# Weighing the scans of two neighbouring Mamba units in one VectorE instruction over two PSUM banks

## The reference, cut to what matters

```python
def step(h, inp):
    dt_t, B_t, C_t, x_t = inp
    dA = jnp.exp(dt_t[..., None] * A)
    h = dA * h + (dt_t * x_t)[..., None] * B_t[:, None, :]
    y = jnp.einsum('ben,bn->be', h, C_t)
    return (h, y)
...
y = ssm_scan(dt, Bm, Cm, xc, A) + xc * Dp
y = y * jax.nn.silu(z)
return jnp.einsum('ble,de->bld', y, outproj)
```

## Time and profile before

| what | value |
|---|---|
| median of 3 runs | 2925.25 us |
| the 3 runs | 2925.6, 2925.25, 2921.18 us |
| span of the profiled execution, first to last instruction | 2927.1 us |
| mean granted TensorE clock over the span | 0.944 |
| busy: PE, DVE, ACT, POOL | 84%, 64%, 46%, 52% |
| weighings on VectorE (L581) | 624, 419.8 us |

### The profile page before, as it was taken

The page is one execution under the profiler, slowest core; times in us unless marked ns, Lnnn a source line. Parts: engine busy times, 40 slices in busy tenths (PEclk is TensorE's granted clock), DMA queues, the critical chain, the costliest instruction groups (busy, mean ns, idle before and its releaser), DMA issues. The chain is left out here.

```text
span 2927.1 us, 26112 instructions
## 1 busy us (share of the span) xinstructions
PE 2456.1 (84%) x8044; PEld 1106.1 (38%) x8044; DVE 1872.1 (64%) x2521; ACT 1332.9 (46%) x2087; POOL 1530.9 (52%) x1340
## 2 busy tenths in 40 slices
PE   7989989889897788688888549999588989778978
PEld 3333323333332233333333338888332333223322
DVE  2999999999999933466663400000239999994334
ACT  4656466565664433345555212222056565542333
POOL 2999999999999811500000230000439999982010
PEclk9999999999999999899999669999689999999989
DMA  4031230321203000612310324444230320300000
GB/s 186 1 115 47 94 117 1 122 70 55 115 1 115 0 21 17 141 24 33 45 23 1 138 106 181 177 175 175 79 155 1 116 94 24 115 1 20 0 9 29
DMA packets 72193, 215.12 MB, mean 73 GB/s; under 512 B 14044, under 2 KB 39271, under 8 KB 53495
## 3 DMA queue, kind: packets, MB, share of 16 engines
q1 hardware_dynamic: 65380, 180.85, 18.9%
q10 hardware_dynamic: 3602, 24.22, 2.5%
q0 software_dynamic: 3072, 8.39, 0.9%
HBM read 187.80 MB, written 25.43 MB: 73 GB/s over the span
## 5 line engine op out<-in xcount | busy, mean ns | idle before, releaser
L895 POOL TENSOR_TENSOR s_dbu<-s_dx,s_bc 128x512 f32<-128x512 f32 x768 | 967.8, 1284 | 47.9 <-DVE s_psum L561 44.1
L480 PE MATMUL s_psum<-s_hc,ident 128*128 128x512 f32 x1536 | 832.2, 632 | 181.2 <-DVE s_hc L581 170.2
L764 ACT ACTIVATE s_psum<-s_dt,s_a_neg 128x512 f32<-128x512 f32 x768 | 521.6, 688 | 590.5 <-DVE s_hc L581 589.5
L480 PEld LDWEIGHTS s_psum<-s_hc,ident 128*128 128x128 f32 x1536 | 257.9, 192 | 695.2 <-DVE s_hc L581 505.4
L581 DVE TENSOR_TENSOR s_hc<-s_psum,s_bc 128x512 f32<-128x512 f32 x624 | 419.8, 673 | 0.6 <-PE s_psum L480 0.4
L561 DVE TENSOR_TENSOR_SCAN s_psum<-s_psum,s_state,s_dbu 128x512 f32<-128x512 f32 x312 | 395.1, 1277 | 18.5 <-ACT s_psum L764 12.7
L561 DVE TENSOR_TENSOR_SCAN s_psum<-s_psum,s_dbu 128x512 f32<-128x512 f32 x312 | 381.3, 1222 | 22.0 <-ACT s_psum L764 13.8
L1968 ACT ACTIVATE s_probs<-s_banks 128x512 f32<-128x512 f32 (+3 forms) x384 | 169.2, 493 | 149.5 <-PE s_banks L1693 107.0
L2381 POOL DMA_INDIRECT s_rows_in<-moe_out_rows,s_place x32 | 30.6, 957 | 357.0 <-DMA moe_out_rows<-s_ys 347.5
L2360 ACT ACTIVATE s_hidden<-s_banks,s_w 128x256 f32<-128x256 f32 x184 | 77.1, 470 | 300.9 <-PE s_banks L2183 300.9
L163 POOL TENSOR_TENSOR s_pair<-s_res 128x512 f32<-128x512 f32 x4 | 5.0, 1265 | 386.1 <-issue 384.6
(11 more groups left out here) (306 smaller groups left out, 3320.6 us busy)
## 6 DMA issues: line engine op xcount, KB each, us to landing
s_bc<-fwd_rows SPq DMA_DIRECT2D x64, 1024.0 KB, 4.7
s_bc<-m_rows SPq DMA_DIRECT2D x32, 1024.0 KB, 4.7
s_w<-in_moe_w SPq DMA_DIRECT2D x23, 1028.0 KB, 7.2
s_w<-in_moe_w ACTq DMA_DIRECT2D x23, 1024.0 KB, 5.5
qk_parts<-s_parts SPq DMA_DIRECT2D x48, 128.0 KB, 1.9
s_stack_q<-qk_parts SPq DMA_DIRECT2D x48, 128.0 KB, 4.5
s_stack_k<-qk_parts SPq DMA_DIRECT2D x48, 128.0 KB, 7.6
moe_in_rows<-s_zero SPq DMA_DIRECT2D x1, 5888.0 KB, 18.8
```

The lines of the kernel that those rows point to most:

```text
L480: pe.matmul(psum[:, SCANS + block_no % 2, :], consts["ident"][:], hc[:, unit % PRODUCTS, :], start=(n == 0), stop=(n == NS - 1)).then_inc( ...
L764: act.activation(psum[:, unit % SCANS, :], dt[:, g % 2, i // NS, :], ACT.Exp, scale=a_neg[CHUNKS[g][0]][:, i:i + 1]).then_inc(decay_ready, 1)
L895: pool.tensor_tensor(dbu[:, unit % TERMS, :], dx[:, g % 2, i // NS, :], bc[:, 2 * n, :], ALU.mult)\
```

## The change

VectorE no longer weighs each unit behind the scan that follows it. It does so only behind the scans of even units i. If unit i - 2 is lent, it weighs unit i - 1 alone as before; if not, one new instruction (`weigh_two`, L593 of the changed kernel) weighs units i - 2 and i - 1 together: 2 x 512 columns from two neighbouring PSUM banks, times two rows of C, into two neighbouring buffers `hc`. It raises `product_ready` by 2 when it is done. Of 64 units 12 are lent, 12 are weighed alone and 40 in 20 pairs; over 12 groups 240 pairs take the place of 480 single weighings, and 144 single ones stay.

```diff
+            def weigh_two(unit):
+
+                n = unit % NS
+                dve.wait_ge(scanned, unit + 2)
+                if unit % UNITS < NS:
+                    dve.wait_ge(row_loaded[n // 2], 16 * (unit // UNITS + 1))
+                if unit + 1 >= PRODUCTS:
+                    dve.wait_ge(product_used, unit + 1 - PRODUCTS + 1)
+                at, to = unit % SCANS, unit % PRODUCTS
+                dve.tensor_tensor(hc[:, to:to + 2, :], psum[:, at:at + 2, :], bc[:, 2 * n + 1:2 * n + 4:2, :], ALU.mult)\
+                   .then_inc(product_ready, 2)
+
+            def weigh_before(unit):
+
+                if LENT[(unit - 2) % UNITS]:
+                    weigh(unit - 1)
+                else:
+                    weigh_two(unit - 2)
+
...
-                    if unit and not LENT[(unit - 1) % UNITS]:
-                        weigh(unit - 1)
+                    if unit and unit % 2 == 0:
+                        weigh_before(unit)
...
-            weigh(NC * UNITS - 1)
+            weigh_before(NC * UNITS)
```

## The result

The changed kernel takes 2965.45 us (median of 4 runs, 2959.79 to 2971.01), the kernel before 2925.43 (4 runs, 2921.18 to 2928.88): a ratio of 1.0142 with a 95% interval of 1.0130 to 1.0154, 40 us slower. The forecast was 29 us slower, 2954 us, in a range of 2939 to 2966. The profiled execution is the fastest of the four, 2959.79 us with a span of 2957.7.

What follows compares the result with a forecast made beforehand. VectorE sets the pace, but in bound chains the end of the first weighing counts. Terms 18.7 + 6.8 + 5.7 + 3.5 - 7.2 + 1.2 = +28.7 us on 2925.25 give 2954 us, range 2939 to 2966.

Steps and rivals of the forecast that it cites:

- Chain B: Scans 37 to 45 (S37, S45): decay 40 waits for pair (36, 37), starting 1.70 us later in 11 groups; +18.7 us.
- Chain C: Scans 52 to 56 (S52, S56): decay 55 and all behind it come 0.62 us later in 11 groups; +6.8 us.
- chain A: Scans 19 to 23 (S19, S23): decay 20 runs ahead of 21, delaying it 0.63 us in 9 groups; +5.7 us.
- GpSimd's place: Scans 0 to 10, where GpSimd sets the time: a weighing carried past scan 10 costs 0.35 us in 10 groups; +3.5 us.
- S56 to the next S0: Stretch from scan 56 to the next group's scan 0: counted pairs save 0.05 us each; -3.0 us.
- What a pair saves: On VectorE, a pair takes 1.135 us against 1.18 to 1.20 for two single weighings: 0.05 us saved.
- busy time falls by about 30 us: Sign of being right: VectorE's busy time falls about 30 us while its waits for L764 grow from 26.5 to some 70.
- Edits at nothing: Effects costed at zero, first TensorE: a pair waits for `product_used` of an addition that TensorE finished 2 us before.
- the end of the calls: Units 62 and 63 are weighed together, so TensorE's last addition comes 0.6 us later in each of two calls; +1.2 us.
- faster: Rival: VectorE's saved time passes to the end, gaining 12 us (2913 us, chance 0.05) or 31 us (2894 us, 0.02).
- the pair is not slow: Rival denied here: each pair lasts two full durations, 1.35 us, adding 19 us and 4 us; 2977 us, chance 0.04.
- from somewhere I have not seen: Sign of being wrong: the groups lengthen but the wait of scan 45 (S45) does not; no size given.

## Why the prediction was right and wrong

- *Chain B*, +18.7: right. +19.7 in the profile, +19.2 alone. Decay 40 starts 1.70 us later behind S37, and S45 waits 4.11 us, 4.2 forecast. In groups 2 and 6 the stretch grows by 2.13 instead of 1.64, for a reason in the last section.
- *Chain C*, +6.8, and *chain A*, +5.7: right in the mechanism. S56 waits 1.91 us and S23 0.70, as said. Group 2 hides A in part (+0.19); in group 9 C shows at S56 (+0.95) and is given back by the next S0 (-0.97). That A's sum is +6.0 is partly luck: group 4 alone has +1.50, with matmuls at the lower clock ahead of that S23. In the runs without chain B and with the residual added later, which have the same pairs here, it has +0.51, and the sum is +5.0.
- *GpSimd's place*, +3.5: right in sum (+2.6 with the savings, +2.3 forecast).
- *S56 to the next S0*, -3.0, is near by luck: -0.27 us in odd groups is the saving of five pairs, but two terms that the prediction doesn't have cancel there, the weighing carried past S56 and the one of unit 62 passed on to the next group. In groups 7 and 11, which pass nothing on, the stretch to S63 grows by 0.33.
- *What a pair saves*, 0.05: right. VectorE's busy time fell from 1872.1 to 1859.3 us: 12.8 us over 240 pairs, 0.053 each. With 180 pairs (all chains taken out) it fell by 9.8, with 120 by 6.3: 0.054 and 0.053. By durations it would be 2 x 673 - 1201 = 145 ns. The prediction's sign "busy time falls by about 30 us" took durations where its own text said that starts count; the busy time of the page counts overlapping tails once, and 12 was the number to write. The rule of the Trainium skill that the prediction weighed ("VectorE: DVE Perf Modes", errata section and rules for kernel authors) would by estimate have given 38 us: it fits the durations (1224 ns by it, 1201 measured), not the time that is saved.
- **The step that failed is the first of "Edits at nothing"**: TensorE "waits for products most of the time here, has done it 2 us before". That was read off for `product_used`, where it holds (0.9 us of waits for 240 pairs), and then taken for TensorE as a whole. TensorE's own products come later too, and up to unit 23 it has 1.72 us of work for each 1.68 us of VectorE's. Who waits for TensorE was never asked; it is the addition of the residual, 0.5 to 0.9 us in six groups and 2.4 in group 7, of which the lower clock makes 1.76. That is +5.9 instead of -1.8, 7.7 us. Without it the sum would be near 32; with it the time comes to the very edge of the range of 2939 to 2966 (the median is 2965.45, and 1.0142 of the 2925.25 that the forecast started from is 2966.8). The runs that tell it apart are those with 11 and 10 pairs: one pair in a group less, and the 7.3 us are gone.
- The other 3.5 us are chain B (+1.0), S56 to the next S0 (+0.9), chain C (+0.7), and 0.3 each in A, in GpSimd's place and at the end of the calls. The group that was said to take 120.8 us takes 121.55, with 0.75 of it at the residual.
- Against the rivals: nothing of "faster" was seen, and the pair is not slow. The warning sign that the prediction named last, a delay "from somewhere I have not seen", came true beside the forecast rather than in its place.

## What to carry to other kernels

Joining two instructions that free buffers moves the release of the first to the end of the second, so cost it at the engine that waits for the buffer, not at the engine that gets rid of an instruction: here 13 us saved cost 53 (12.8 + 39.9). Do the walk for every consumer of what is delayed, and for those who wait for that consumer, and compare the work per unit of each engine within the stretch rather than over the group. Where a joined instruction can be put so that it ends before the release that starts a long chain, the same instruction wins.

## What was not expected of the hardware

**TensorE's clock falls with bunched work.** The windows view over the two calls, before (66 to 1018, 2180 to 2642) and, in the second fence, after (65 to 1045, 2200 to 2672):

```profile
66.00:1018.00 952.00, 827.67 (x1730) 303.79 (x1728) 913.63 (x1114) 552.28 (x760) 896.73 (x770) 0.98 0.19 68
2180.00:2642.00 462.00, 392.30 (x806) 139.19 (x804) 447.65 (x548) 257.39 (x356) 436.68 (x377) 0.98 0.16 59
```

```profile
65.00:1045.00 980.00, 825.82 (x1728) 325.63 (x1726) 904.16 (x955) 542.51 (x760) 898.54 (x770) 0.95 0.18 67
2200.00:2672.00 472.00, 388.68 (x804) 152.41 (x802) 443.32 (x469) 253.35 (x357) 438.21 (x378) 0.95 0.16 58
```

The granted clock goes from 0.98 to 0.95. The loss comes in bursts at the lower level, 1.2 GHz, most of them close behind a wait of TensorE for a weighing. Such a burst in group 2 of the changed kernel (granted clock 0.50 from 382 to 388), in TensorE's timeline, and what it does to VectorE's:

```profile
380.45 1.27 PE L480 MATMUL s_psum<-s_hc,ident 128*128 128x512 f32 x2 [1.26 <-DVE s_hc L593]
382.45 2.05 PE L498 MATMUL s_psum<-s_dx,ones 128*128 128x512 f32 x2 [0.73 <-ACT s_pad L748]
384.29 1.91 PE L480 MATMUL s_psum<-s_hc,ident 128*128 128x512 f32 x2
...
386.34 1.22 DVE L593 TENSOR_TENSOR s_hc<-s_psum,s_bc 128x1024 f32<-128x1024 f32 x1 [0.38 <-PE s_psum L480]
```

Two matmuls take 2.05 us instead of 1.02, the pair waits 0.38 us for its buffer, and decay 44 with it: that is the 0.48 us by which S37 to S45 is longer in groups 2 and 6. The Trainium skill ("TensorE: Matmul & The Clock Gate", "HAM oscillation") describes a clock that falls when the engine pauses between groups of matmuls; the trace agrees, with 0.98 against 0.95. Beside this 0.48 us in two groups it cost 1.76 us in group 7, read above; no run isolates what the clock alone costs in all.

**An instruction of VectorE with both inputs in SBUF can take five times its length beside GpSimd**: `scale_y` from 0.75 to 1.78 and 4.06 us, on average over 16 of them 1208 ns before and 1828 in the kernel that starts chain B earlier. The Trainium skill ("SBUF — State Buffer", "Who interferes with whom") says that such an instruction contends with one of GpSimd that reads SBUF, calls the ports that the two share an exclusive lock, and has the issue order decide who blocks. The rows fit that, and show more: VectorE's instruction ended not behind one of GpSimd's (1.24 us) but behind three in a row; that it was kept out for all three is read from these times and no run isolates it. An S45 that came 1.2 us earlier so cost 2.66 us behind it, and no row of the kernel before tells it.
